# Attention scores of two heads in the two 64-row halves of the array, in phases by query block

## The chip, the cores and the metric

The kernel runs on one core of one Trainium2 chip. The metric is the device time of one execution in microseconds (us). Lower is better.

## What is computed

One block of a transformer: cross-attention with a residual, then a layer of mixed experts with a residual, over 2048 rows of 512. Only the first part matters here. Its rows are channels: `q.reshape(B, 8, 64, 512)` makes every 64 rows one head.

```python
def _L0_xattn_ref(q, k, v, gamma):       # q = layernorm(x), k = v = ctx_2048; B = 4, Dq = 512, L = 512
    h = 8; dq = Dq // h; dv = Dv // h    # 64 channels to a head
    qh, kh, vh = (a.reshape(B, h, 64, 512) for a in (q, k, v))
    qk = einsum('bhdq,bhdl->bhql', qh, kh) / sqrt(64)
    sm = softmax(qk, axis=-1)
    ret = einsum('bhql,bhdl->bhdq', sm, vh).reshape(B, Dv, Lq)
    return gamma * ret
x = x + _L0_xattn_ref(_layernorm(x), ctx_2048, ctx_2048, gamma)
x = x + _L0_ffn_ref(_layernorm(x), router_w, w_gate, w_up, w_down, sw_gate, sw_up, sw_down, shared_gate_w)
```

`_L0_ffn_ref` is a shared expert of width 1408 and the two best of eight experts of width 352.

## The kernel before

**Tiles.** The attention works on 16 tiles of 128 rows. A tile `t` holds two heads, `s` = 0 and 1, of 64 rows each; `k = 2 * t + s` counts heads. The scores of a head are 512 queries by 512 keys: four blocks of 128 queries, each filling one PSUM bank (`bS[0]` to `bS[3]`). After the attention come the shared expert (from about 282 us in the trace) and the routed experts (39 slots); the change leaves both as they are.

**Precision.** Operands of matmuls are fp32r. To keep precision each factor is split into a high and a low part (`kh`, `kl` of the keys; high and low of the queries; `vs[.., 0/1]` of the values; `pth`, `ptl` of the transposed probabilities).

**Scores before.** Each head uses all 128 rows of the array. `qs[s]` holds the high queries in one half of its rows and the low ones in the other; `cd` holds the keys of each head twice, once in each half, and is loaded by two DMAs per tile (L342), on top of the load of `cn`, the same rows in natural layout, from which the values come (L346). Per query block two matmuls of 512 columns are enough: `qs` with `kh` (L1234) and `qs` with `kl` (L1235). That is 16 for a tile, in four groups of four.

**One tile, engine by engine.** Every engine has its own queue, written out by hand in a function `tile`, and works through it in order; an engine stops at a semaphore wait, and with it all that is behind.
- PE (L1297 to L1329): for each head and each `c` of four 128-key chunks, `probs_T` transposes four 128x128 blocks of probabilities into `bT[c % 2]` (L1242), and `times_v` adds three matmuls into `bO` (L1255, L1256, L1258). The groups of scores of the next tile stand between them, and so do `values_T`, `rows_T` (four transposes each) and `logits` (eight narrow passes).
- DVE (L977 on): `maxima` (L925) takes the row maximum of each score bank, `inverse` (L930) the reciprocal of the sums, `probs_lo` (L934) makes `ptl` from `bT` and `pth`, `values_lo` (L918) the low part of the values, `rows_out` (L940) adds the finished attention to the rows, and `bn_stats` (L897) takes the moments.
- ACT (L718 on): `exps` (L681) makes the probabilities from a score bank, `probs_hi` (L687) copies `bT` to `pth`, `values_hi` (L673) and `rows_T` (L693) copy out of `bM`, `normed` makes `xn` (L657) and `x2n` (L661), and `queries_hi` (L668) the high queries, 64 rows at a time.
- POOL (L562 on): `norm_p` (L550) multiplies the probabilities by the reciprocal, `keys_hi` and `keys_lo` (L540, L544) split 128x1024 of keys, `queries_lo` (L533) makes the low queries of a head, and `power` (L521, L523) the scale and shift of a normalisation.
- SP (L401 on) issues the loads and stores of the rows.

**Phases.** In the kernel before, the scores of the next head are made while the present head is transposed and multiplied. Each `pb[s]` (the probabilities of one head, four query blocks) exists once. `probs_T` reads columns of all four query blocks, so the first one of a head waits until `norm_p` has done all four blocks of that head (L1239).

## Time and profile before

| | us |
|---|---|
| median of 3 runs | 990.9 (988.89 to 993.4) |
| span of the profiled execution, first to last instruction | 980.4 |
| what the median has above this span | 10.5 |
| attention, until the first matmul of the shared expert | 281.7 |
| one tile of the attention in the steady part | 15.9 |
| PE busy in the span | 887.9 (91%) |

The profile is of one execution. Its own time by the clock that the median uses isn't given; the difference of 10.5 us between the median and its span is what lies around the span. A row of the timeline gives the start, the duration, the engine, the line, what is written and read, and how many instructions were merged; in brackets stands for how long the engine sat idle before it and what released it. PE's matmuls overlap: a row lasts longer than the time to the next one's start, and the distance of the starts is the rate. On ACT and DVE, too, an instruction starts some 0.1 us before the row ahead of it ends.

### The profile page before, as it was taken

The page shows a single profiled execution, that of the slowest core. Times are in us where ns is not written, and L with a number is a line of the kernel's source. Part 1 is how long each engine was busy: PE and PEld are TensorE (multiplying, and loading weights), DVE is VectorE, ACT ScalarE, POOL GpSimd, SP SyncE. Part 2 cuts the span into 40 slices and gives each one's busy share as a digit, 9 for nine tenths or more (in the row PEclk, how much of TensorE's full clock was granted, in tenths as well). Part 3 has the DMA queues.
Part 4 walks back from the last instruction along what each step waited for, and adds up shares of the span by engine and source line. Part 5 has one row for each costly group of instructions (what it writes and reads, how often), then busy time and mean ns, then how long its engine had stood idle before and what let it go on. Part 6 is the DMA issues. An engine that isn't in the chain of part 4 may idle for free.

```text
span 980.4 us, 14857 instructions
## 1 busy us (share of the span) xinstructions
PE 887.9 (91%) x4560; PEld 743.1 (76%) x4560; DVE 608.1 (62%) x920; ACT 537.9 (55%) x918; POOL 487.4 (50%) x500
## 2 busy tenths in 40 slices
PE   5798999989989999999999999999888888888993
PEld 3587777778777888888888888888777777777882
DVE  5678787878845633421222121258999998999881
ACT  5588878787855321121121111258777777777781
POOL 5687788777610000273100000027777778887774
PEclk9899999999999999999999999999999999999996
DMA  9334434443633323000400055556333333333333
GB/s 138 80 127 132 134 125 137 120 148 109 226 120 117 97 76 128 1 1 25 118 11 1 0 175 177 177 176 209 66 65 64 64 64 64 64 64 64 65 55 43
DMA packets 70143, 93.78 MB, mean 96 GB/s; under 512 B 16137, under 2 KB 35593, under 8 KB 70098
## 3 DMA queue, kind: packets, MB, share of 16 engines
q1 hardware_dynamic: 60338, 72.73, 24.9%
q0 software_dynamic: 9760, 20.49, 12.1%
q8 instruction: 24, 0.39, 0.2%
q14 instruction: 21, 0.17, 0.1%
HBM read 65.59 MB, written 27.60 MB: 95 GB/s over the span
## 4 chain that ended last, share of the span: by engine, by line
PE 43%; POOL 15%; issue 13%; ACT 2%; POOLq 2%; DMA 2%; DVE 1%; SPq 0%; ACTq 0%; DVEq 0%
PE bank L1348 8%; PE bank L1349 8%; PE bank L1350 8%; POOL sidx L615 5%; POOL wd L631 4%; PE bank L1362 4%; PE bank L1364 4%; PE bank L1363 4%; POOL gidx L607 2%; POOL out L624 2%; POOL xg L610 1%; DMA out<-y,sidx 1%; PE bank L1242 1%; ACT pb L681 1%; PE bank L1415 1%
## 5 line engine op out<-in xcount | busy, mean ns | idle before, releaser
L1036 DVE TENSOR_TENSOR sg<-bank,sg 128x512 f32<-128x512 f32 x44 | 30.4, 692 | 208.7 <-PE bank L1350 200.0
L1348 PE MATMUL bank<-x_hl,wsp 128*128 128x512 f32 x352 | 137.1, 390 | 0.0
L1350 PE MATMUL bank<-x_hl,wsp 128*128 128x512 f32 x352 | 137.0, 389 | 0.0
L1349 PE MATMUL bank<-x_hl,wsp 128*128 128x512 f32 x352 | 136.9, 389 | 0.0
L610 POOL DMA_INDIRECT xg<-x_normed_rows,gidx x39 | 40.9, 1048 | 186.9 <-PE bank L1372 158.8
L1152 DVE TENSOR_TENSOR wg<-wex,wg 128x1408 fp32r<-128x1408 f32 x39 | 112.0, 2871 | 12.4 <-ACT wg L813 12.4
L624 POOL DMA_INDIRECT out<-y,sidx x39 | 96.0, 2462 | 38.4 <-POOL sidx L615 18.4
L787 ACT ACTIVATE sg<-bank 128x512 f32<-128x512 f32 x44 | 26.3, 598 | 158.4 <-PE bank L1350 158.4
L687 ACT ACTIVATE pth<-bank 128x512 fp32r<-128x512 f32 x128 | 73.3, 598 | 49.2 <-PE bank L1242 47.7
L593 POOL DMA_INDIRECT slot_rows<-msrc,posi x32 | 32.8, 1025 | 134.2 <-DVE posi L1143 124.7
L934 DVE TENSOR_TENSOR ptl<-bank,pth 128x512 fp32r<-128x512 f32 x128 | 85.9, 682 | 18.7 <-ACT pth L687 18.4
L550 POOL TENSOR_SCALAR pb<-pb,rinv 128x512 f32<-128x512 f32 x128 | 87.3, 696 | 13.3 <-DVE rinv L930 7.8
L794 ACT ACTIVATE hh<-sg 128x512 fp32r<-128x512 f32 x44 | 27.8, 631 | 114.9 <-DVE sg L1036 100.2
L681 ACT ACTIVATE pb<-bank,negmax 128x512 f32<-128x512 f32 x128 | 86.9, 689 | 0.7 <-DVE negmax L925 0.3
L925 DVE TENSOR_REDUCE negmax<-bank 128x1 f32<-128x512 f32 x128 | 82.2, 682 | 0.8 <-PE bank L1235 0.2
L1234 PE MATMUL bank<-kh,qs 128*128 128x512 f32 x128 | 58.8, 459 | 20.7 <-POOL qs L533 17.1
L1350 PEld LDWEIGHTS bank<-x_hl,wsp 128*128 128x128 f32 x352 | 66.1, 188 | 13.7
L1348 PEld LDWEIGHTS bank<-x_hl,wsp 128*128 128x128 f32 x352 | 66.1, 188 | 13.7
L1349 PEld LDWEIGHTS bank<-x_hl,wsp 128*128 128x128 f32 x352 | 66.1, 188 | 13.6
L1242 PE MATMUL bank<-ident,pb 128*128 128x128 f32 x512 | 72.4, 275 | 2.8 <-POOL pb L550 2.8
L848 ACT ACTIVATE wd<-wex 128x1024 fp32r (+1 forms) x39 | 41.3, 1060 | 60.1 <-PE bank L1441 59.3
L1242 PEld LDWEIGHTS bank<-ident,pb 128*128 128x128 f32 x512 | 61.9, 142 | 14.1 <-POOL pb L550 3.8
(160 smaller groups left out, 2420.0 us busy)
## 6 DMA issues: line engine op xcount, KB each, us to landing
cd<-in_ctx SPq DMA_DIRECT2D x32, 256.0 KB, 4.9
wex<-in_L_ffn_w_gate SPq DMA_DIRECT2D x8, 704.0 KB, 4.4
wex<-in_L_ffn_w_up SPq DMA_DIRECT2D x8, 704.0 KB, 5.8
xb<-in_x SPq DMA_DIRECT2D x16, 256.0 KB, 4.7
cn<-in_ctx SPq DMA_DIRECT2D x16, 256.0 KB, 3.0
x2b<-in_x SPq DMA_DIRECT2D x16, 256.0 KB, 2.7
x_rows<-x2b SPq DMA_DIRECT2D x16, 256.0 KB, 2.1
x_normed_rows<-x2n SPq DMA_DIRECT2D x16, 256.0 KB, 2.0
```

The lines of the kernel that those rows point to most:

```text
L550: gp.tensor_scalar(pb[s][:, q, :], pb[s][:, q, :], rinv[:, s, q:q + 1], 0.0, ALU.mult, ALU.add).then_inc(g_pn, 1)
L624: g.indirect_dma_start(out=out, out_offset=bass.IndirectOffsetOnAxis(ap=sidx[j % 4][:, 0:1], axis=0), in_=y3[j % 2][:, :], in_offset=None, ...
L681: sc.activation(pb[s][:, q, :], bS[q][:, :], ACT.Exp, bias=negmax[:, s, q:q + 1], scale=1.0, accum_out=rsum[:, s, q:q + 1]).then_inc(a_exp, 1)
L687: sc.activation(pth[c][:, :], bT[c % 2][:, :], ACT.Copy).then_inc(a_pth, 1)
L925: ve.tensor_reduce(negmax[:, s, q:q + 1], bS[q][:, :], AX_X, ALU.max, negate=True).then_inc(d_max, 1)
L934: ve.tensor_tensor(ptl[c][:, :], bT[c % 2][:, :], pth[c][:, :].bitcast(F32), ALU.subtract).then_inc(d_ptl, 1)
L1152: ve.tensor_tensor(wg3[:, 1, :], wex[:, e, 0:W3], wg3[:, 0, :].bitcast(F32), ALU.subtract).then_inc(d_wg, 1)
L1234: te.matmul(bS[q][:, :], qs[s][:, q * P:(q + 1) * P], kh[par][:, s, :], start=True, stop=False)
L1242: ins = te.transpose(bT[c % 2][:, q * P:(q + 1) * P], pb[s][:, q, c * P:(c + 1) * P], ident[:, :])
L1348: te.matmul(bk[:, :], hi, xhi, start=(h == 0), stop=False)
L1349: te.matmul(bk[:, :], hi, xlo, start=False, stop=False)
L1350: ins = te.matmul(bk[:, :], lo, xhi, start=False, stop=(h == HC - 1))
```

## The change

The scores of both heads are made together, one query block `c` at a time. `kh`, `kl`, `qh` and `ql` hold 128 rows in natural layout, rows 0 to 63 for head 0 and rows 64 to 127 for head 1. A group of scores is six matmuls with 64 contracted rows each: high by high, high by low, low by high, each first for head 0 in the upper rows and then for head 1 in the lower rows, into two banks `bS[2 * (c % 2) + s]`. There are 24 in a tile, in four groups of six. `cd` and its two DMAs per tile are gone; `kh` and `kl` come from `cn` and are 128x512 instead of 128x1024. `xn` is now one buffer, made on POOL (`queries`) instead of ACT; ACT makes `qh` in one 128x512 instruction directly from `xb`, and POOL makes `ql` in one 128x512 instruction. `pb` exists twice for each head, so that a whole tile can be prepared ahead. `negmax`, `rsum` and `rinv` are indexed by query block and then head. `exps`, `maxima`, `inverse` and `norm_p` take the two heads of a query block, and their places in the queues are new; SP issues the load of `cn` for tile `t + 2` first in a tile, ahead of the stores, instead of last.

In the diff below the removed lines of the functions `tile` of POOL, ACT, DVE and PE are left out (they stand in the listing above), as are declarations, the start-up ahead of the first tile, and the definitions that only follow the new shapes.

```diff
                 if there(t + 2):
+                    load_values(t + 2, par)
                     load_x(t + 2, par)
-                    load_keys(t + 2, par)
                 if there(t - 2):
                     store_columns(t - 2, par)
                 if there(t - 1):
                     store_rows(t - 1, 1 - par)
                 if there(t + 1):
                     load_x2(t + 1, i + par, 1 - par)
-                if there(t + 2):
-                    load_values(t + 2, par)
...
+            def queries(t, par):
+
+                wait_ahead(g, g_nmr[0], t + 1)
+                gp.tensor_scalar(xn[:, :], xb[par][:, :], rstd[:, 0, :], nmr[:, 0, :], ALU.mult, ALU.add).then_inc(g_xn, 1)
+
+            def queries_lo(t, par):
+
+                wait_ahead(g, g_xn, t + 1)
+                g.wait_ge(a_qh, t + 1)
+                gp.tensor_tensor(ql[par][:, :], xn[:, :], qh[par][:, :].bitcast(F32), ALU.subtract).then_inc(ql_done, 1)
+                wait_ahead(g, ql_done, t + 1)
...
+            def norm_p(t, par, c):
+
+                wait_ahead(g, d_rinv, 4 * t + c + 1)
+                for s in range(2):
+                    gp.tensor_scalar(pb[par][s][:, c, :], pb[par][s][:, c, :], rinv[:, c, s:s + 1], 0.0,
                                      ALU.mult, ALU.add).then_inc(g_pn, 1)
...
             def tile(t, i, par):
+                if there(t + 1):
+                    norm_p(t + 1, 1 - par, 0)
                 if there(t + 2):
                     keys_hi(t + 2, i + 1, par)
                 if there(t - 1):
                     power(1, t - 1)
                 if there(t + 1):
+                    norm_p(t + 1, 1 - par, 1)
                 if there(t + 2):
                     power(0, t + 2)
+                    keys_lo(t + 2, par)
+                if there(t + 1):
+                    norm_p(t + 1, 1 - par, 2)
                 if there(t + 2):
+                    queries(t + 2, par)
+                    queries_lo(t + 2, par)
+                if there(t + 1):
+                    norm_p(t + 1, 1 - par, 3)
...
+            def queries_hi(t, par):
+
+                act.wait_ge(g_nmr[0], t + 1)
+                after(act, e_s, 8 * t - 8)
+                after(act, ql_done, t - 1)
+                sc.activation(qh[par][:, :], xb[par][:, :], ACT.Identity, bias=nmr[:, 0, :], scale=rstd[:, 0, :]).then_inc(a_qh, 1)
...
+            def exps(t, par, c):
+                after(act, e_t, 8 * t - 8)
+                for s in range(2):
+                    act.wait_ge(d_max, 8 * t + 2 * c + s + 1)
+                    sc.activation(pb[par][s][:, c, :], bS[2 * (c % 2) + s][:, :], ACT.Exp, bias=negmax[:, c, s:s + 1], scale=1.0,
+                                  accum_out=rsum[:, c, s:s + 1]).then_inc(a_exp, 1)
...
                 k = 2 * t
                 probs_hi(k, 0)
                 probs_hi(k, 1)
                 if there(t - 2):
                     rows_T(t - 2, i - 1, par)
                 if there(t + 1):
+                    exps(t + 1, 1 - par, 0)
                 probs_hi(k, 2)
+                if there(t + 1):
+                    exps(t + 1, 1 - par, 1)
                 probs_hi(k, 3)
+                if there(t - 2):
+                    logits(t - 2)
                 if not there(t + 1):
                     tokens_hi(0, 0)
                 k = 2 * t + 1
                 probs_hi(k, 0)
+                if there(t - 1):
+                    rows_normed(t - 1, i - 1 + par, 1 - par)
+                if there(t + 1):
+                    exps(t + 1, 1 - par, 2)
+                if there(t + 2):
+                    queries_hi(t + 2, par)
                 probs_hi(k, 1)
                 if not there(t + 1):
+                    act.wait_ge(a_qh, NT)
+                    act.wait_ge(g_xn, NT)
                     act.wait_ge(e_vt, NT)
                     act.wait_ge(kl_done, NT)
+                    act.wait_ge(e_s, 8 * NT)
                     weights_hi(0)
                 if there(t + 1):
+                    values_hi(t + 1, 1 - par)
                 probs_hi(k, 2)
                 if there(t + 1):
+                    exps(t + 1, 1 - par, 3)
                 probs_hi(k, 3)
                 if not there(t + 1):
                     weights_hi(1)
...
+            def maxima(t, c):
+                for s in range(2):
+                    dve.wait_ge(e_s, 8 * t + 2 * c + s + 1)
+                    ve.tensor_reduce(negmax[:, c, s:s + 1], bS[2 * (c % 2) + s][:, :], AX_X, ALU.max, negate=True).then_inc(d_max, 1)
+
+            def inverse(t, c):
+                dve.wait_ge(a_exp, 8 * t + 2 * c + 2)
+                after(dve, g_pn, 8 * t + 2 * c - 6)
+                ve.reciprocal(rinv[:, c, :], rsum[:, c, :]).then_inc(d_rinv, 1)
...
 
             def tile(t, i, par):
                 k = 2 * t
+                if isinstance(t, int) and t == 0:
+                    inverse(0, 3)
                 if there(t - 1):
                     rows_out(t - 1, i - 1 + par, 1 - par)
                 probs_lo(k, 0)
+                if there(t + 1):
+                    maxima(t + 1, 0)
                 if there(t - 1):
                     dve.wait_ge(d_x2, t)
                     moments(1, t - 1, x2b[1 - par][:, :])
                 probs_lo(k, 1)
                 if there(t - 1):
                     aggregate(1, t - 1)
                 if there(t + 1):
+                    inverse(t + 1, 0)
+                    maxima(t + 1, 1)
                 if there(t - 1):
                     variance(1, t - 1)
                 probs_lo(k, 2)
...
                 probs_lo(k, 3)
                 if not there(t + 1):
                     tokens_lo(0, 0)
+                if there(t + 1):
+                    inverse(t + 1, 1)
                 if there(t + 2):
                     aggregate(0, t + 2)
                 k = 2 * t + 1
+                probs_lo(k, 0)
                 if there(t + 2):
                     variance(0, t + 2)
                 if there(t + 1):
+                    maxima(t + 1, 2)
                 probs_lo(k, 1)
                 if there(t + 1):
+                    values_lo(t + 1, 1 - par)
+                    inverse(t + 1, 2)
+                    maxima(t + 1, 3)
                 probs_lo(k, 2)
                 if not there(t + 1):
                     weights_lo(0)
                 if there(t + 1):
+                    inverse(t + 1, 3)
                 probs_lo(k, 3)
                 if not there(t + 1):
                     weights_lo(1)
...
-            def scores(k, t, par, s, pair):
-
-                if pair == 0:
-                    pe.wait_ge(ql_done, k + 1)
+            def scores(t, par, c):
+
+                if c == 0:
+                    pe.wait_ge(ql_done, t + 1)
                     pe.wait_ge(kl_done, t + 1)
 
-                after(pe, a_exp, 4 * k - 4 + 2 * pair + 2)
-                for q in (2 * pair, 2 * pair + 1):
-                    te.matmul(bS[q][:, :], qs[s][:, q * P:(q + 1) * P], kh[par][:, s, :], start=True, stop=False)
-                    te.matmul(bS[q][:, :], qs[s][:, q * P:(q + 1) * P], kl[par][:, s, :], start=False, stop=True).then_inc(e_s, 1)
-
-            def probs_T(k, s, c):
+                after(pe, a_exp, 8 * t + 2 * c - 2)
+                terms = ((qh, kh), (qh, kl), (ql, kh))
+                for n, (a, b) in enumerate(terms):
+                    for s in range(2):
+                        r = slice(DH * s, DH * (s + 1))
+                        ins = te.matmul(bS[2 * (c % 2) + s][:, :], a[par][r, c * P:(c + 1) * P], b[par][r, :], start=(n == 0), stop=(n == 2))
+                        if n == 2:
+                            ins.then_inc(e_s, 1)
+
+            def probs_T(k, par, s, c):
                 if c == 0:
-                    pe.wait_ge(g_pn, 4 * k + 4)
+                    pe.wait_ge(g_pn, 4 * k + 7 if s == 0 else 4 * k + 4)
                 after(pe, d_ptl, 4 * k + c - 1)
                 for q in range(QC):
-                    ins = te.transpose(bT[c % 2][:, q * P:(q + 1) * P], pb[s][:, q, c * P:(c + 1) * P], ident[:, :])
+                    ins = te.transpose(bT[c % 2][:, q * P:(q + 1) * P], pb[par][s][:, q, c * P:(c + 1) * P], ident[:, :])
                 ins.then_inc(e_t, 1)
...
             def tile(t, i, par):
                 k = 2 * t
+                probs_T(k, par, 0, 0)
+                probs_T(k, par, 0, 1)
+                if there(t + 1):
+                    scores(t + 1, 1 - par, 0)
                 times_v(k, t, 0, par, 0)
+                probs_T(k, par, 0, 2)
+                if there(t + 1):
+                    scores(t + 1, 1 - par, 1)
                 times_v(k, t, 0, par, 1)
+                probs_T(k, par, 0, 3)
                 if there(t - 2):
                     logits(t - 2, par)
                 times_v(k, t, 0, par, 2)
                 k = 2 * t + 1
+                probs_T(k, par, 1, 0)
+                if there(t + 1):
+                    scores(t + 1, 1 - par, 2)
+                times_v(k - 1, t, 0, par, 3)
+                if there(t + 1):
+                    values_T(t + 1, i + par, 1 - par)
+                probs_T(k, par, 1, 1)
                 times_v(k, t, 1, par, 0)
+                probs_T(k, par, 1, 2)
+                if there(t + 1):
+                    scores(t + 1, 1 - par, 3)
                 times_v(k, t, 1, par, 1)
+                probs_T(k, par, 1, 3)
                 times_v(k, t, 1, par, 2)
                 if there(t - 1):
                     rows_T(t - 1, 1 - par)
```

## Rows read from the trace of the kernel before

**Rows 1.** The page, busy time of PE over the span, its share and instructions.
```profile
PE 887.9 (91%) x4560; PEld 743.1 (76%) x4560; DVE 608.1 (62%) x920; ACT 537.9 (55%) x918; POOL 487.4 (50%) x500
```
**Rows 2.** Windows: stretch, its length, busy us of each engine, clock, DMA share, GB/s.
```profile
150.00:200.00 50.00, 46.22 (x274) 38.82 (x273) 40.79 (x88) 41.98 (x97) 40.55 (x50) 1.00 0.41 131
```
**Rows 3.** Timeline of PE, one tile from its first transposes to the next one's.
```profile
153.44 1.03 PE L1242 MATMUL bank<-ident,pb 128*128 128x128 f32 x8
155.60 0.49 PE L1234 MATMUL bank<-kh,qs 128*128 128x512 f32 x1 [1.13 <-POOL qs L533]
155.93 0.39 PE L1235 MATMUL bank<-kl,qs 128*128 128x512 f32 x1
...
156.63 0.39 PE L1255 MATMUL bank<-pth,vs 128*128 128x512 f32 x1
...
157.32 0.60 PE L1242 MATMUL bank<-ident,pb 128*128 128x128 f32 x4
157.67 0.48 PE L1255 MATMUL bank<-pth,vs 128*128 128x512 f32 x1
...
159.81 0.95 PE L1282 MATMUL bank<-rgT,x2T 128*128 128x9 f32 x8
160.62 0.48 PE L1255 MATMUL bank<-pth,vs 128*128 128x512 f32 x1
...
169.38 1.04 PE L1242 MATMUL bank<-ident,pb 128*128 128x128 f32 x8
```
**Rows 4.** Timeline of ACT in the same stretch.
```profile
158.03 0.60 ACT L687 ACTIVATE pth<-bank 128x512 fp32r<-128x512 f32 x1 [0.31 <-PE bank L1242]
...
166.29 0.62 ACT L673 ACTIVATE vs<-bank 128x512 fp32r<-128x512 f32 x1
166.80 0.60 ACT L687 ACTIVATE pth<-bank 128x512 fp32r<-128x512 f32 x1
167.30 0.81 ACT L657 ACTIVATE xn<-xb,nmr,rstd 128x512 f32<-128x512 f32 x1
168.00 0.68 ACT L681 ACTIVATE pb<-bank,negmax 128x512 f32<-128x512 f32 x1
...
168.67 0.69 ACT L681 ACTIVATE pb<-bank,negmax 128x512 f32<-128x512 f32 x1
```
**Rows 5.** Timeline of DVE just behind it.
```profile
169.56 0.17 DVE L930 RECIPROCAL rinv<-rsum 128x2 f32<-128x2 f32 x1 [1.01 <-ACT pb L681]
169.68 1.29 DVE L925 TENSOR_REDUCE negmax<-bank 128x1 f32<-128x512 f32 x2
170.89 0.74 DVE L940 SCALAR_TENSOR_TENSOR x2b<-bank,gam,x2b 128x512 f32<-128x512 f32 x1
171.54 0.68 DVE L934 TENSOR_TENSOR ptl<-bank,pth 128x512 fp32r<-128x512 f32 x1
172.14 0.69 DVE L897 BATCH_NORM_STATS2 stats<-x2b 128x6 f32<-128x512 f32 x1
```
**Rows 6.** Timeline of POOL in the tile of rows 3.
```profile
158.42 1.36 POOL L550 TENSOR_SCALAR pb<-pb,rinv 128x512 f32<-128x512 f32 x2
...
160.91 1.29 POOL L533 TENSOR_TENSOR qs<-xn,qs 64x512 fp32r<-64x512 f32 x1 [0.18 <-POOL nmr L523]
162.41 0.55 POOL L521 TENSOR_TENSOR rstd<-vare,mhalf 128x1 f32<-128x1 f32 x1 [0.21 <-issue]
...
164.70 2.38 POOL L544 TENSOR_TENSOR kl<-cd,kh 128x1024 fp32r<-128x1024 f32 x1
```
**Rows 7.** Timelines: first transposes of tiles 0, 1 and 15; POOL's wait in tile 0.
```profile
20.70 1.09 PE L1242 MATMUL bank<-ident,pb 128*128 128x128 f32 x8 [0.92 <-POOL pb L550]
...
30.55 1.04 POOL L540 TENSOR_SCALAR kh<-cd 128x1024 fp32r<-128x1024 f32 x1 [8.58 <-DMA cd<-in_ctx]
...
41.50 1.03 PE L1242 MATMUL bank<-ident,pb 128*128 128x128 f32 x8
...
266.30 1.03 PE L1242 MATMUL bank<-ident,pb 128*128 128x128 f32 x8
```

220 lines of the change are left out of this document (61 added, 159 removed).

## The prediction, made before the change ran

> **What bounds the kernel now.** I read the page first: PE is busy for 91% of the span [rows 1], so at first sight any matmul saved is time saved. But the change touches only the attention, so that stage has to be read alone. In its steady part PE has 46.2 of 50 us, and DVE, ACT and POOL 40 to 42 each, at a granted clock of 1.00 [rows 2]: four engines stand within some 15% of each other, and then the order of the queues matters as much as the sums. So I went to the timelines. A tile takes 169.38 - 153.44 = 15.94 us [rows 3]. Eight transposes take 0.79 us until the next matmul can start (two groups of four at 0.35, and 0.09), yet the scores start at 155.60, which is 1.37 us later than that: PE waits for the low queries from POOL. PE's own work is 15.94 - 1.37 = 14.57 us per tile. So the present bound is PE, plus one stall that POOL causes.
>
> **Durations taken from the rows**, as the distance of starts. PE [rows 3]: four transposes 0.35; a 512-column matmul 0.23 (0.32 for the first behind transposes); `times_v` 0.69; a group of scores 156.63 - 155.60 = 1.03; `logits` 0.81; a result is there 0.40 after the start of its last matmul. From the start of four transposes to ACT's copy 158.03 - 157.32 = 0.71. ACT [rows 4]: a copy 0.50, a scaled 128x512 copy 0.70, `exps` 0.67 for one head and 1.33 for a pair; the reciprocal can start 169.56 - 168.67 = 0.89 after the second exp's start [rows 4, 5]. DVE [rows 5]: a pair of maxima 1.20, `rows_out` 0.65, a subtraction or statistics 0.60 (its result after 0.69), small ones 0.1. POOL [rows 6]: `norm_p` of two blocks 1.36, a subtraction over 512 columns 1.2 to 1.3 (half of the 2.38, or the 64-row one), 0.2 behind each wait on its own result. Hand-overs between engines cost 0.03 to 0.1 us.
>
> **The change, part by part.** (a) Scores on PE. Sixteen full matmuls become 24 half ones. If the halves run side by side, a group is three steps of 0.23 plus 0.09, or 0.78, against 1.03. The trace has no 64-row matmul and no change between halves and the whole array. I bound a change between 0 and 0.17 us: a matmul lasts 0.40 while the next one starts after 0.23 [rows 3], so emptying the array exposes at most 0.17. I take 0.12, since a real change seems nearer to emptying than to nothing, and two of them per group: a group is 0.78 to 1.12, taken as 1.0. Were the halves one after the other it would be 6 x 0.23 + 0.09 = 1.47, and up to 1.8 with changes. So PE's own work becomes about 14.45 us: this part alone gives almost nothing. (b) The stall of 1.37 us goes, because `ql` of a tile is now made a whole tile ahead. (c) POOL loses about 0.5 + 1.2 us (keys at half the width) and about 1.3 (one `ql` for two), and gains `queries` at 0.68. (d) ACT loses `xn` and two half copies and gets `qh`: 0.70 against some 1.95. (e) DVE has the same work, in another order. (f) Two DMAs of 256 KB per tile go. The load of `cn` moves to the head of SP's queue, past two stores of rows, the store of columns and `load_x2`; it waits there for `e_vt` and `kl_done` of the previous tile, both long past, and behind it only the load of `xb` is queued. The data are first used in the next tile, so this is hidden. In total PE, ACT and POOL all get less to do. The question is what the new order does.
>
> **The walk through one steady tile after the change**, with the first transposes of head 0 at time 0, in the order of the new queues and with the durations above. PE: transposes c0 at 0 and c1 at 0.35, scores block 0 at 0.79 with the result at 1.97, `times_v` c0 at 1.79, transposes c2 2.48, scores block 1 at 2.83 (result 4.0), `times_v` c1 from 3.83. DVE: `rows_out`, `ptl` c0 at 1.33, maxima of block 0 at 1.97 to 3.17, statistics to 3.77, `ptl` c1 to 4.37 (result 4.46), aggregate, reciprocal 0 to 4.55, maxima 1 to 5.75, variance, `ptl` c2 at 5.82 (result 6.51). The last matmul of `times_v` c2 needs it, so it starts at 6.54, and head 1's first transposes at 6.77. ACT copies them at 7.47 to 8.10, DVE subtracts to 8.70 and takes the maxima of block 2 from 8.77 to 9.97 (first result 9.46). ACT now has `exps` 2 from 9.49 to 10.82, then `qh` to 11.52, and only then the copy of head 1's c1, which is there at 12.15. **DVE waits for that copy from 9.97 to 12.15**, because `probs_lo` stands next in its queue; behind it stand `values_lo`, reciprocal 2 and maxima 3. `ptl` c1 to 12.75, `values_lo` to 13.35, reciprocal 2 to 13.44, maxima 3 to 14.64, `ptl` c2 to 15.33. ACT: `exps` 3 from 14.16 to 15.49 and head 1's last copy to 16.12; `ptl` c3 is done at 16.81, the last matmul of the tile starts at 16.84, and PE is free at 17.07. That is one end. POOL has another: `norm_p` 2 waits for reciprocal 2, 13.53 to 14.87; `queries` to 15.6; 0.2; `queries_lo` to 17.0; 0.2; and only then `norm_p` 3, whose first half ends at 17.9. The next tile's first transposes wait for exactly that (seventh `g_pn` of the tile). **So the period is 17.95 us**, 2.0 more than now, with three chains above 15.94: POOL's (17.95), the tile's last `ptl` (17.07), and `exps` 3 directly to `norm_p` 3 without the queries (reciprocal at 15.72, 16.5).
>
> The Trainium skill (TensorEngine Tiling (Array Packing), Key Properties) says that a change of tiling mode drains TensorE. Priced by the row bound of 0.17 for each of the two changes in a group, the two groups ahead of head 1's transposes would put the period near 18.15 and the time near 1016. No run here shows it yet.
>
> **The sum.** Tile 0's first transposes stay near 20.7 [rows 7]. The scores start some 3 us earlier, since `kh` no longer waits for `cd`, but all four query blocks of both heads must then be through exps and `norm_p`: eight exps and seven of eight `norm_p` at 0.67 to 0.68, with `ql` of tile 1 (1.4), `queries` (0.7) and `keys_lo` (1.2) between them, about the same end. Tile 0 now takes 41.50 - 20.70 = 20.8 us, with POOL waiting 8.58 us for `cd` [rows 7]; after the change 1 MB less lies ahead of that load and its data are wanted only about 6 us into the tile, so I take the pure 17.95 and little stall, and tile 1 starts near 38.5: 3.0 us gained (0 to 4). Thirteen tiles (1 to 13) of 17.95 are 233.4, and tile 14, which has no queries of a tile 16 in its queues, about 16.3: tile 15 starts at 288.2 instead of 266.30 [rows 7], 21.9 later. Tile 15 has no scores ahead; I leave it and all behind it as they are (0 to 1 us less). The span becomes 980.4 + 22 = 1002, and with the 10.5 us around it the time is 1013 us, 2.2% above the median of 990.9.
>
> **The rivals.** (1) PE sets the pace and the chains above don't hold. For: PE is the busiest engine now, ACT and POOL get lighter, and the stall goes. The period is then 13.6 (changes free) to 14.5. Against: every link of the walk is an order in a queue. It decides if the copy of head 1's c1 and the last `ptl` come 2.5 us earlier than I have them. Time: 14 x (14.5 - 15.94) - 3 = -23, so 968 us. (2) The halves do not run side by side, so the change doesn't do what it says on PE. A group is 1.5 to 1.8; the two groups ahead of head 1's transposes push these by 1.0 us and the rest follows; period 18.9. Time: 1013 + 13 x 0.95 = 1025 us. No row excludes it. The skill speaks for overlap: the page TensorE: Matmul & The Clock Gate, Part 3, reports 3.07 times for four tiles of 32 rows at 512 columns; by it the group would stay at or below my 1.0. No row of this trace can confirm that. (3) POOL's chain is too long in my walk (the queries finish earlier), and the tile's last `ptl` sets the period at 17.07: 13 x -0.88, so 1001 us. (4) About no change: two chains are over-priced by a microsecond each and the period is 16.0 to 16.3: 988 to 995 us.
>
> **Chances.** The forecast (1005 to 1020) 0.48, (2) and above 0.18, (3) 0.14, (4) 0.08, (1) 0.12. A measurement of this kernel tells about 0.5%, 5 us, from no change. So faster by more than that 0.12, within it 0.08, slower 0.80. For 8 in 10 I leave out (1) and the far end of (2): 988 to 1028.
>
> **What would show each step.** In the profile after: the distance of the first transposes of tiles (17.9 right, 14.5 rival 1, 17.1 rival 3); PE idle before the first transposes of a tile, released by `norm_p`, and before `times_v`, released by `pth` and `ptl`; DVE idle before `ptl` about 2 us per tile, released by ACT; the wait of PE on the low queries gone; the starts of two matmuls of a pair of scores within 0.1 us of each other and pairs 0.23 apart (rival 2: every matmul 0.23 apart); the gap behind a group of scores (a change of mode); a period with less idle time on DVE than 4 us would refute the walk. The prediction would also be wrong if PE's longer pauses (up to 1.6 us by the walk) lowered its granted clock: it is 1.00 now with pauses of 1.4 us, and a fall would make the tile longer still.

## The result, and the profile after

The changed kernel takes 1028.9 us (median of 4 runs, 1025.8 to 1034.0), the kernel before it 992.2 us beside it: a ratio of 1.037, interval 1.033 to 1.042. A later comparison gave 1.033 (1.031 to 1.035). So it is slower by some 33 to 37 us, where 22 us were forecast. The profiled execution has a span of 1032.0 us and a time of 1034.0.

The page first: the row that answers to [rows 1].

```profile
PE 920.8 (89%) x4688; PEld 727.1 (70%) x4688; DVE 612.5 (59%) x918; ACT 520.2 (50%) x886; POOL 459.5 (45%) x502
```

ACT and POOL have less work in all, 18 and 28 us, as the change says, and yet the kernel is slower. PE's busy time is up by 33 us although its work is about the same. Short waits disappear in the modelled ends of matmuls (from 166.25 to 166.64 us the timeline of PE has one step of 0.39 where a step is 0.23, and no idle time beside it), so a PE that is kept waiting a little all the time looks busy. In this one execution PE also paused in the shared expert, with 3.92 us busy and a granted clock of 0.52 from 480 to 490 us; the repeated run of the changed kernel has no such pause, so it is not the change's. The stretch of [rows 2] (same columns) says more:

```profile
150.00:200.00 50.00, 44.12 (x260) 30.55 (x261) 36.10 (x78) 32.78 (x79) 29.29 (x44) 1.00 0.21 73
```

Every engine was less busy in these 50 us, at a granted clock of 1.00: PE 44.1 for 46.2, DVE 36.1 for 40.8, ACT 32.8 for 42.0, POOL 29.3 for 40.6. Nobody is the bound; everybody waits. For whom, the table of waits tells (engine and line that waited, line that it waited for, us in total, times, longest; stretch of 75 to 295 us, twelve tiles):

```profile
POOL pb L542 <- DVE rinv L912: 83.4, 36, 4.3
DVE ptl L916 <- ACT pth L675: 49.1, 48, 2.2
...
ACT pb L669 <- DVE negmax L907: 33.3, 48, 1.1
...
PE bank L1229 <- POOL pb L542: 11.0, 12, 1.0
```

PE's wait for POOL's low queries, the stall of 1.13 us in [rows 3], is gone. In its place stands a ring: POOL waits for DVE's reciprocals, DVE for ACT's copy, ACT for DVE's maxima, and PE, at the head of each tile, for POOL. The timelines show one turn of it (start, duration, engine, line, operation, count, idle time before and its releaser). PE, from a tile's first transposes to the next one's:

```profile
153.54 1.09 PE L1229 MATMUL bank<-ident,pb 128*128 128x128 f32 x8 [0.99 <-POOL pb L542]
...
156.25 0.60 PE L1229 MATMUL bank<-ident,pb 128*128 128x128 f32 x4
156.78 0.50 PE L1220 MATMUL bank<-kh,qh 64*128 64x512 f32 x2
157.11 0.39 PE L1220 MATMUL bank<-kl,qh 64*128 64x512 f32 x2
157.34 0.40 PE L1220 MATMUL bank<-kh,ql 64*128 64x512 f32 x2
157.67 0.50 PE L1242 MATMUL bank<-pth,vs 128*128 128x512 f32 x1
...
169.09 0.51 PE L1245 MATMUL bank<-ptl,vs 128*128 128x512 f32 x1 [1.04 <-DVE ptl L916]
...
172.10 1.09 PE L1229 MATMUL bank<-ident,pb 128*128 128x128 f32 x8 [1.00 <-POOL pb L542]
```

A tile takes 172.10 - 153.54 = 18.56 us, for 15.94 in [rows 3]. The scores do go in pairs, three steps of 0.33, 0.23 and 0.33 us. But the group costs 157.67 - 156.78 = 0.89, and the way into it 156.78 - 156.25 = 0.53 where four transposes gave way after 0.35 in [rows 3]. That is 0.18 us for going into the 64-row mode and, 0.89 against my 0.78, 0.11 for coming out of it: 1.07 in all, against 1.03 for a group before. By the records the packing gives nothing on PE.

ACT, DVE and POOL in the second half of the same tile:

```profile
163.90 0.68 ACT L669 ACTIVATE pb<-bank,negmax 128x512 f32<-128x512 f32 x1
...
164.56 0.81 ACT L650 ACTIVATE qh<-xb,nmr,rstd 128x512 fp32r<-128x512 f32 x1
165.27 0.59 ACT L675 ACTIVATE pth<-bank 128x512 fp32r<-128x512 f32 x1
```
```profile
162.51 1.28 DVE L907 TENSOR_REDUCE negmax<-bank 128x1 f32<-128x512 f32 x2
165.89 0.69 DVE L916 TENSOR_TENSOR ptl<-bank,pth 128x512 fp32r<-128x512 f32 x1 [2.10 <-ACT pth L675]
166.50 0.68 DVE L901 TENSOR_TENSOR vs<-bank,vs 128x512 fp32r<-128x512 f32 x1
167.10 0.16 DVE L912 RECIPROCAL rinv<-rsum 128x2 f32<-128x2 f32 x1
167.17 1.27 DVE L907 TENSOR_REDUCE negmax<-bank 128x1 f32<-128x512 f32 x2
```
```profile
167.43 1.36 POOL L542 TENSOR_SCALAR pb<-pb,rinv 128x512 f32<-128x512 f32 x2 [2.19 <-DVE rinv L912]
168.77 0.76 POOL L519 TENSOR_SCALAR xn<-xb,rstd,nmr 128x512 f32<-128x512 f32 x1
169.68 1.28 POOL L525 TENSOR_TENSOR ql<-xn,qh 128x512 fp32r<-128x512 f32 x1
171.27 1.36 POOL L542 TENSOR_SCALAR pb<-pb,rinv 128x512 f32<-128x512 f32 x2 [0.31 <-POOL ql L525]
```

On ACT the second exp of block 2 and the high queries stand ahead of the copy of head 1's second transposes. DVE idles 2.10 us for that copy. The reciprocal of block 2, an instruction of 0.16 us whose input was ready near 164.8, stands two places further down and starts at 167.10. POOL idles 2.19 us for it, then does `norm_p` 2, the queries, the low queries and only at 171.27 `norm_p` 3, for which PE waits.

The start of tiles 0, 1 and 15, for [rows 7]:

```profile
20.91 1.97 PE L1229 MATMUL bank<-ident,pb 128*128 128x128 f32 x8 [4.97 <-POOL pb L542]
...
41.08 1.97 PE L1229 MATMUL bank<-ident,pb 128*128 128x128 f32 x8 [0.41 <-POOL pb L542]
...
300.06 1.03 PE L1229 MATMUL bank<-ident,pb 128*128 128x128 f32 x8
```

Tile 15 starts 33.8 us later than before, and the shared expert behind the attention starts 35.3 us later (317.0 for 281.7). That is the size of the whole measured loss. The spans of the two profiled executions differ by more, 51.6 us: 16.3 of them lie behind the attention, where both kernels run the same code (715.0 us for 698.7). In the repeated run of the changed kernel that part took 701.4, and in the other runs of this document, all with the same code there, 696 to 716. So I don't count it as the change's. In the repeated run the shared expert starts at 313.3, 31.6 later than before.

### The profile page after: what moved, and what is told of

Read it like the earlier page. It is cut to its first block, busy times and chain, and to the rows that moved or that the text cites. A ratio compares the mean times of both kernels' runs of the same rounds, so it can differ in the third digit from the quotient of the medians.

```text
span 1032.0 us, 14928 instructions
## 1 busy us (share of the span) xinstructions
PE 920.8 (89%) x4688; PEld 727.1 (70%) x4688; DVE 612.5 (59%) x918; ACT 520.2 (50%) x886; POOL 459.5 (45%) x502
## 4 chain that ended last, share of the span: by engine, by line
PE 39%; POOL 14%; issue 13%; DMA 2%; POOLq 2%; ACT 1%; DVE 1%; SPq 0%; DVEq 0%; ACTq 0%
PE bank L1335 8%; PE bank L1337 8%; PE bank L1336 8%; POOL sidx L608 5%; POOL wd L624 4%; PE bank L1349 4%; PE bank L1351 4%; PE bank L1350 4%; POOL gidx L600 2%; POOL out L617 2%; DMA out<-y,sidx 1%; POOL xg L603 1%; PE bank L1229 1%; POOLq L624 0%; DMA stg<-in_L_ffn_sw_down 0%
## 5 line engine op out<-in xcount | busy, mean ns | idle before, releaser
L1335 PE MATMUL bank<-x_hl,wsp 128*128 128x512 f32 x352 | 139.1, 395 | 3.9 <-issue 3.7
L1337 PE MATMUL bank<-x_hl,wsp 128*128 128x512 f32 x352 | 138.7, 394 | 2.7 <-issue 2.7
L1336 PE MATMUL bank<-x_hl,wsp 128*128 128x512 f32 x352 | 138.8, 394 | 1.4 <-issue 1.3
L603 POOL DMA_INDIRECT xg<-x_normed_rows,gidx x39 | 40.8, 1046 | 187.3 <-PE bank L1359 159.3
L1135 DVE TENSOR_TENSOR wg<-wex,wg 128x1408 fp32r<-128x1408 f32 x39 | 116.7, 2992 | 12.6 <-ACT wg L796 12.6
L1229 PE MATMUL bank<-ident,pb 128*128 128x128 f32 x512 | 78.1, 282 | 16.9 <-POOL pb L542 16.9
L1229 PEld LDWEIGHTS bank<-ident,pb 128*128 128x128 f32 x512 | 64.0, 145 | 31.7 <-issue 13.5
L1335 PEld LDWEIGHTS bank<-x_hl,wsp 128*128 128x128 f32 x352 | 67.0, 190 | 18.9 <-issue 5.3
L1337 PEld LDWEIGHTS bank<-x_hl,wsp 128*128 128x128 f32 x352 | 66.9, 190 | 17.2 <-issue 3.3
L1336 PEld LDWEIGHTS bank<-x_hl,wsp 128*128 128x128 f32 x352 | 67.0, 190 | 17.0 <-issue 3.2
L1245 PE MATMUL bank<-ptl,vs 128*128 128x512 f32 x128 | 56.8, 444 | 17.7 <-DVE ptl L916 17.7
```

The source lines that it names most:

```text
L1135: ve.tensor_tensor(wg3[:, 1, :], wex[:, e, 0:W3], wg3[:, 0, :].bitcast(F32), ALU.subtract).then_inc(d_wg, 1)
L1229: ins = te.transpose(bT[c % 2][:, q * P:(q + 1) * P], pb[par][s][:, q, c * P:(c + 1) * P], ident[:, :])
L1245: te.matmul(bO[:, :], hi, ptl[c][:, :], start=False, stop=last).then_inc(e_pv, 1)
L1335: te.matmul(bk[:, :], hi, xhi, start=(h == 0), stop=False)
L1336: te.matmul(bk[:, :], hi, xlo, start=False, stop=False)
L1337: ins = te.matmul(bk[:, :], lo, xhi, start=False, stop=(h == HC - 1))
```

## The experiments

To size the steps I repeated the walk of the prediction for several tiles in a row, with every duration from this trace: changes of mode 0.18 and 0.11, a hand-over of 0.2 us to POOL and 0.04 to the others, the low queries 1.28 and 0.31 behind them. It gives 18.49 us per tile for the changed kernel, and the name "queue walk" below means this sum for other orders of the queues. The period of a kernel is read off as the mean distance of `queries` on POOL over three to five tiles near 150 us. Each ratio is against the kernel before, timed on the same chip.

**Do the halves depend on the order of issue?**

```diff
-                for n, (a, b) in enumerate(terms):
-                    for s in range(2):
+                for s in range(2):
+                    for n, (a, b) in enumerate(terms):
```

> The changed kernel with one difference: the six matmuls of a group of scores go out as three of head 0 and then three of head 1, so that neighbours share their 64 rows and only one pair of six can overlap. Everything else stays. If halves overlap only when neighbours differ (my reading of pairs starting together), a group grows from 0.89 us by 0.37 to 0.46 us, and by the walk through the queues the tile grows from 18.5 by about 0.65 us: about +9 us, 1038 us. Rival (TensorE's own work is what made the change slow): four groups cost their full 1.5 to 1.8 us per tile, +21 to +26 us, 1050 us or more. If order does not matter to the overlap: no change.

Ratio 1.035 (1.029 to 1.041), period 18.57: no change. The timeline of PE shows the reason:

```profile
151.24 0.50 PE L1220 MATMUL bank<-kh,qh 64*128 64x512 f32 x2
151.58 0.40 PE L1220 MATMUL bank<-kl,qh 64*128 64x512 f32 x2
151.81 0.40 PE L1220 MATMUL bank<-kh,ql 64*128 64x512 f32 x2
152.14 0.50 PE L1242 MATMUL bank<-pth,vs 128*128 128x512 f32 x1
```

Although the three matmuls of head 0 are issued ahead of the three of head 1, the records still show them in pairs, and the group still takes 0.90. That the other order reached the chip shows in one thing: the two starts of a pair are 10 nanoseconds apart in the records of this run, in the median, and 3 in the changed kernel. So this gave no serial control; that took another kernel.

**What is the overlap worth?** Both heads' six matmuls in rows 0 to 63:

```diff
-                        r = slice(DH * s, DH * (s + 1))
+                        r = slice(0, DH)
```

> The changed kernel, but the scores of both heads use rows 0 to 63 of the operands (head 1's scores are left out, head 0's stand in both places), so the six matmuls of a group share one half of the array and cannot run side by side. Issue order, banks and all waits stay. If the halves really run in parallel in the changed kernel, a group now takes six steps of 0.23 us instead of three, 0.69 us more, so the distance from the first transposes of one tile to the next goes from 18.56 to about 20.1 us (queue walk with a group of 1.79 us instead of 1.10), and the time rises by about 14 x 1.5 = 21 us, to a ratio near 1.058 against the kernel before. Rival: the pairs of the changed kernel only look simultaneous in the records and the array is shared in time: then the starts go on in steps as they are now, and period and time stay at 18.56 and 1.037. Second rival: two matmuls into the same rows also run side by side because each uses half the rows: same outcome as the first rival, but with pairs still starting together.

```profile
152.41 0.72 PE L1220 MATMUL bank<-kh,qh 64*128 64x512 f32 x2
152.97 0.62 PE L1220 MATMUL bank<-kl,qh 64*128 64x512 f32 x2
153.44 0.63 PE L1220 MATMUL bank<-kh,ql 64*128 64x512 f32 x2
153.99 0.51 PE L1242 MATMUL bank<-pth,vs 128*128 128x512 f32 x1
```

No two matmuls of this group start together in the records. The group takes 1.58 instead of 0.89, the period is 19.95 us and the ratio 1.060 (1.058 to 1.062), 26 us above the changed kernel beside it. The overlap of the halves is real. The second rival of the prediction priced its absence at 0.95 us a tile; it costs 1.39.

**Are the changes of mode what is lost?** In the changed kernel's own order, a group of scores as four matmuls over 128 rows:

```diff
-                terms = ((qh, kh), (qh, kl), (ql, kh))
+                terms = ((qh, kh), (ql, kh))
...
-                        ins = te.matmul(bS[2 * (c % 2) + s][:, :], a[par][r, c * P:(c + 1) * P], b[par][r, :], start=(n == 0), stop=(n == 2))
+                        ins = te.matmul(bS[2 * (c % 2) + s][:, :], a[par][:, c * P:(c + 1) * P], b[par][:, :], start=(n == 0), stop=(n == 1))
```

> The changed kernel in its own order, with each group of scores as four matmuls over the whole 128 rows, as in the kernel before, instead of six over 64 rows (the products mix the heads and the middle term is left out, so the scores are not those of the reference). It prices the change of mode and the packing where the queues set the pace. Theory: a group of 1.03 without a change of mode instead of 1.07 with one moves every transpose by less than 0.1 us, and the chain through ACT's copy, DVE's wait, the reciprocal and POOL has its own length: queue walk 18.49 in both cases, so 18.4 to 18.6 us a tile and a ratio of 1.030 to 1.037. Rival: the changes of mode push the two groups ahead of head 1's transposes late and so make 0.2 of the 0.6 us by which a tile exceeds the forecast, then 18.3 to 18.4 and 3 us less; or they are worth more than the records of PE show, and the period falls towards the forecast 17.95.

```profile
157.30 0.60 PE L1228 MATMUL bank<-ident,pb 128*128 128x128 f32 x4
157.66 0.71 PE L1219 MATMUL bank<-kh,qh 128*128 128x512 f32 x2
158.20 0.63 PE L1219 MATMUL bank<-kh,ql 128*128 128x512 f32 x2
158.67 0.39 PE L1241 MATMUL bank<-pth,vs 128*128 128x512 f32 x1
```

From the transposes to `times_v` it is 158.67 - 157.30 = 1.37 us, for 157.67 - 156.25 = 1.42 with the pairs. The period is 18.49 for 18.56, the ratio 1.031 (1.028 to 1.034). Here it makes next to no difference how the scores are computed (0.07 us of the 2.6 that a tile lost): the loss does not lie in the packing.

**The order of the three lighter engines' queues.** Four edits of the changed kernel, each in one queue.

(1) `norm_p` of block 3 ahead of the queries, on POOL:

```diff
-                if there(t + 2):
-                    queries(t + 2, par)
-                    queries_lo(t + 2, par)
-                if there(t + 1):
-                    norm_p(t + 1, 1 - par, 3)
+                if there(t + 1):
+                    norm_p(t + 1, 1 - par, 3)
+                if there(t + 2):
+                    queries(t + 2, par)
+                    queries_lo(t + 2, par)
```

> The changed kernel with norm_p of query block 3 moved ahead of queries and queries_lo in POOL's queue. My prediction held that POOL's chain (queries, queries_lo, then norm_p 3) sets the period and that without it the next end is 0.9 us earlier: tile 17.6, about -13 us, 1016 us. The rival, from the walk with the trace of the changed kernel: the low queries are wanted by the first scores right at the start of the next tile, so they only move the wait from the transposes to the scores, and the tile gets 19.0 us: +7 us, 1036 us, with PE idle before the scores, released by ql.

Ratio 1.040 (1.034 to 1.045), period 18.8 us. The wait did not go away, it changed its object:

```profile
151.92 1.03 PE L1228 MATMUL bank<-ident,pb 128*128 128x128 f32 x8
154.34 0.50 PE L1219 MATMUL bank<-kh,qh 64*128 64x512 f32 x2 [1.38 <-POOL ql L525]
```

The transposes come on time and the scores behind them wait for the low queries. Those are needed right behind the first eight transposes, so POOL's chain up to the queries has to end early, whatever the order of its last two steps.

(2) The queries ahead of `norm_p` of block 2, where POOL stands idle anyway:

```diff
-                if there(t + 1):
-                    norm_p(t + 1, 1 - par, 2)
-                if there(t + 2):
                     queries(t + 2, par)
                     queries_lo(t + 2, par)
                 if there(t + 1):
+                    norm_p(t + 1, 1 - par, 2)
                     norm_p(t + 1, 1 - par, 3)
```

> The changed kernel with one move, in POOL's queue: queries and queries_lo stand ahead of norm_p of block 2 instead of behind it. They fit into the time in which POOL waits for the reciprocals of block 2. This takes the queries out of the chain reciprocal 2, norm_p 2, queries, queries_lo, norm_p 3, and tests the third rival of the forecast (the last ptl of a tile sets the period). Queue walk: period 17.16 us instead of 18.49, time lower by 14 x 1.33 = 18 us, ratio about 1.019. If PE or the chain through DVE's wait for ACT's copy sets the period by itself, the move gives nothing: 18.5 and 1.037. If queries_lo then holds back norm_p 2 because the high queries come late from ACT, the result lies between.

Ratio 1.020 (1.018 to 1.022), period 17.53: 14 us less than the changed kernel beside it.

(3) One reciprocal, ahead of the `ptl` that waits for ACT's copy:

```diff
+                    inverse(t + 1, 2)
                 probs_lo(k, 1)
                 if there(t + 1):
                     values_lo(t + 1, 1 - par)
-                    inverse(t + 1, 2)
                     maxima(t + 1, 3)
```

> The changed kernel with one instruction of 0.08 us moved in DVE's queue: the reciprocal of block 2 stands ahead of the ptl of head 1's second transposes instead of behind it and values_lo. In the changed kernel it stands behind a ptl that waits for ACT's copy, behind exps 2 and the high queries; norm_p 2, the queries, the low queries and norm_p 3 on POOL all follow it. Theory: without that detour POOL's chain ends 1.9 us earlier and the tile's last ptl sets the period: queue walk 17.08 us instead of 18.49, ratio about 1.018. PE's wait for norm_p ahead of a tile's first transposes should vanish (17 us in all now), DVE's wait for ACT's copy should stay (about 2 us a tile). Rival: DVE's idle time itself, not what is queued behind it, sets the period, then the move gives nothing: 18.5 and 1.033 to 1.037.

Ratio 1.020 (1.016 to 1.025), period 17.46. Moving an instruction of 0.16 us takes 1.1 us off each tile. In the waits (75 to 295 us) PE's wait for POOL has shrunk from 11.0 to

```profile
PE bank L1227 <- POOL pb L542: 0.2, 1, 0.2
```

and DVE's for ACT's copy is 25.0 for 49.1, less than I had expected to remain.

(4) That reciprocal and the maxima of block 3 both ahead of it:

```diff
+                    inverse(t + 1, 2)
+                    maxima(t + 1, 3)
                 probs_lo(k, 1)
                 if there(t + 1):
                     values_lo(t + 1, 1 - par)
-                    inverse(t + 1, 2)
-                    maxima(t + 1, 3)
```

> The changed kernel with two steps moved in DVE's queue: reciprocal 2 and maxima 3 of the next tile go ahead of probs_lo of head 1's chunk 1, into the 2.1 us in which DVE waits for that chunk's copy. PE's work is the same. If the order of the queues is what makes the change slow, the tile falls from 18.5 to about 16.6 us: -27 us, 1002 us. Rival (PE's changes between half and whole array, eight a tile, or the 24 matmuls are the cause): no change beyond 3 us, 1029 us.

Ratio 1.014 (1.009 to 1.020), period about 17.0 us (the walk 16.6). One reciprocal and a pair of maxima further up in one queue give back some 20 of the 33 to 37 us.

**All four queues in another order.** Same instructions, same banks and buffers, no wait left out: POOL does the keys first and the low queries ahead of `norm_p` 3, ACT makes its copies in twos ahead of the exps, DVE takes maxima and reciprocals ahead of the `ptl` that would wait, PE puts a group of scores ahead of a tile's first transposes and the `times_v` of head 1 at the end.

```diff
             def tile(t, i, par):
+                if there(t + 1):
+                    scores(t + 1, 1 - par, 0)
-                k = 2 * t
-                probs_T(k, par, 0, 0)
-                probs_T(k, par, 0, 1)
+                probs_T(2 * t + 0, par, 0, 0)
+                probs_T(2 * t + 0, par, 0, 1)
                 if there(t + 1):
-                    scores(t + 1, 1 - par, 0)
+                    scores(t + 1, 1 - par, 1)
...
```

> The same instructions as the changed kernel, with the queues of DVE, ACT, POOL and PE all put in a new order, so that nothing PE waits for is late: scores and maxima early in the tile, head 0's work in between, values late. If order alone is the cause, the tile comes near PE's own work, 14.9 us by the walk: 14 x -3.6 = -51 us, 978 us, which would be faster than the kernel before by 14 us. Rival (PE's work with the changeovers is already above 15.9 us a tile): not below 992 us.

Ratio 0.987 (0.982 to 0.993), and 0.985 (0.981 to 0.989) in a second comparison, for which I had written:

> The kernel with all four queues reordered again, as the control beside the two built on it, on the same chip: period 15.1 us, ratio 0.985 to 0.99 against the kernel before.

The period is 15.10 in both. By the windows PE never stops:

```profile
150.00:200.00 50.00, 50.00 (x320) 38.45 (x320) 43.92 (x95) 41.19 (x95) 37.49 (x57) 1.00 0.30 106
```

This is the changed kernel faster than the one before, by 1.3 to 1.5%. It also makes PE the bound, so here the price of the scores can be measured in time. Four matmuls over 128 rows in this order (the diff of the scores is the one above):

> The kernel with all four queues reordered (14.85 us by the walk, 15.10 measured), but a group of scores is four matmuls over the whole 128 rows, two per bank, as in the kernel before, instead of six over 64 rows; the operands stay the two heads' natural ones, so the products mix the heads and the middle term is left out: the scores are not those of the reference. It prices the packing where PE sets the pace. Theory: six half matmuls in pairs cost 3 x 0.23 + 0.09 plus 0.18 going in and 0.11 coming out, 1.07 to 1.10 us a group, four whole ones cost 1.03 and no change of mode, so the period falls by 0.2 to 0.3 us, to 14.8 to 14.9, and the time by 3 to 4 us against the same orders with packing: packing alone buys nothing on PE and all of the gain of that kernel comes from the queues. Rival: packing pays on PE by three steps instead of four (0.23 a group): the period rises by 0.9 and the time by 13 us.

Ratio 0.979 (0.974 to 0.983) against 0.985 beside it, period 14.80 against 15.10. The 0.3 us a tile is somewhat more than the 4 x 0.05 = 0.2 read off the records; the rival, that packing pays 0.23 a group, is out. The two ratios' intervals overlap, so that whole matmuls are faster here rests on the periods.

**Fewer changes of mode.** Scores of blocks 0 and 1 back to back, and of 2 and 3, all queues ordered around them:

```diff
-                    scores(t + 1, 1 - par, 0)
...
-                    scores(t + 1, 1 - par, 1)
+                    scores(t + 1, 1 - par, 0)
+                    scores(t + 1, 1 - par, 1)
```

> The groups of scores of query blocks 0 and 1 back to back, and those of 2 and 3 (the four score banks hold two groups), with all four queues ordered anew around them. Only two stretches of 64-row matmuls per tile are left instead of four. If each stretch costs 0.18 us going in and 0.11 us coming out plus 0.09 for its first matmul, PE saves about 2 x 0.38 = 0.76 us a tile: queue walk 14.14 us against 14.85 for single groups, so the period should come to 14.3 to 14.5 (the walk has been 0.2 to 0.4 short), and the time to some 9 us below that of the single groups, ratio 0.975 to 0.98. If the changes of mode cost nothing, PE's work stays as it is and the period cannot fall below 15.0: ratio 0.985 to 0.99. If longer stretches of scores starve ACT and DVE of their transposes, it rises above.

Ratio 0.998 (0.995 to 1.001): the forecast failed. The tiles are of uneven length, most between 15.1 and 17.8 us. PE's records of the scores did what was expected. The waits (75 to 250 us) have one that the walk had not:

```profile
DVE stats L875 <- DMA xb<-in_x: 16.5, 10, 2.3
```

In this order DVE's statistics of the next rows stood first in its queue, and the load of those rows had not landed. My walk had no DMA in it. The next run has the statistics behind the fourth `ptl`. Many other steps of all four queues moved with them (the cut shows the statistics alone), so the run tests the new order as a whole:

```diff
             def tile(t, i, par):
...
-                if there(t + 2):
-                    first_norm(t + 2, i + 1, par)
...
                 probs_lo(2 * t + 0, 3)
...
+                if there(t + 2):
+                    first_norm(t + 2, i + 1, par)
```

> The scores in two stretches of two groups per tile again, but with DVE's statistics of the next rows behind the fourth ptl instead of first in its queue, where in the run before they waited for the load of those rows (16.5 us in all), and the queues ordered again under that condition. Theory: the saving on PE (0.37 us for each two groups put together, as that run's records show) is real and was eaten by that wait: queue walk 14.1 us, so a period of 14.2 to 14.5 against 15.10 for single groups, time 9 to 12 us below these, ratio 0.972 to 0.978. Rival: two groups back to back make ACT and DVE late whatever stands first, since for 1.6 us PE makes no transposes: the period stays above 15.1, the ratio at 0.985 or more.

```profile
160.06 0.50 PE L1212 MATMUL bank<-kh,qh 64*128 64x512 f32 x2
160.40 0.39 PE L1212 MATMUL bank<-kl,qh 64*128 64x512 f32 x2
160.63 0.40 PE L1212 MATMUL bank<-kh,ql 64*128 64x512 f32 x2
160.86 0.39 PE L1212 MATMUL bank<-kh,qh 64*128 64x512 f32 x2
...
161.65 0.50 PE L1234 MATMUL bank<-pth,vs 128*128 128x512 f32 x1
```

Two groups take 161.65 - 160.06 = 1.59, and one way in of 0.18: 1.77 for what cost 2 x 1.07 = 2.14. The period is 14.56 us, the ratio 0.975 (0.972 to 0.978), the fastest of all that ran. 15.10 - 14.56 = 0.54 of the 0.74 expected from two such pairs arrive in the time. Since the rest of the queues differs too, no run shows how much of the 0.54 is the changes of mode, nor that the wait for the load alone had spoiled the run before.

**The start.** Is tile 0 long because PE is slow there? 26 transposes that nobody reads, in PE's idle time before it:

```diff
             scores(0, 0, 3)
+            for w in range(26):
+                te.transpose(bT[0][:, (w % QC) * P:(w % QC + 1) * P], ident[:, :], ident[:, :])
```

> The changed kernel with 26 transposes of the identity, whose result nobody reads, put on PE ahead of tile 0, where PE is idle from 15.9 to 20.9 us. Theory: tile 0 takes 20.2 us instead of the forecast 17.95 because its first 5.8 us of matmuls run at half rate (0.43 us per step instead of 0.23) after that idle stretch; with PE busy, the steps at the start of tile 0 are 0.23 us and tile 1 starts 1 to 2.5 us earlier than 41.1. The total falls by the same 1 to 2.5 us. Rival: tile 0 is long for another cause, such as a wait on a load; then tile 1 starts at 41 as now, whatever the step. A second one: the idle stretch has nothing to do with the rate at which tile 0 begins, and the steps stay at 0.43 us.

with the changed kernel itself as the control:

> The changed kernel itself, as a control beside the three variants on the same chip: ratio 1.037 against the kernel before, tiles 18.56 us apart, tile 0 starting at 20.9 and tile 1 at 41.1 us.

```profile
15.32 3.06 PE L1284 MATMUL bank<-ident 128*128 128x128 f32 x26
21.01 1.09 PE L1229 MATMUL bank<-ident,pb 128*128 128x128 f32 x8 [2.62 <-POOL pb L542]
...
40.18 1.97 PE L1229 MATMUL bank<-ident,pb 128*128 128x128 f32 x8 [0.48 <-POOL pb L542]
```

The control's tile 0 starts at 21.00, with the eight transposes at half rate (1.97 us), and its tile 1 at 40.90. With the warm start the eight transposes go at full rate, but after them the granted clock falls to 0.57 and only at 25.8 are the steps 0.23 again, for 26.5 in the control. PE is at half rate for about 3.8 us of tile 0 instead of about 5.5. By estimate 1.7 us less at half rate are worth half of that, 0.85 us; tile 0 is 19.2 us instead of 19.9, 0.7 us less. Over the whole kernel nothing is left of it: 1.034 (1.031 to 1.038) against 1.033. The profiled execution lost more in tile 1 than it had gained: there its clock fell again, and tile 1 took 20.4 us for 18.0 in the control.

The control differs in one more thing. In it PE is at half rate already ahead of the idle stretch (steps of 0.43 from its first scores at 8.4 us on), while the execution with the warm start had reached the full rate at 12.4, before the added transposes. The run with `norm_p` 3 first, which starts as the changed kernel does, had the full rate from 12.2 us on too, and after its idle stretch it was at half rate:

```profile
14.80 0.40 PE L1219 MATMUL bank<-kh,ql 64*128 64x512 f32 x2
20.83 1.97 PE L1228 MATMUL bank<-ident,pb 128*128 128x128 f32 x8 [5.64 <-POOL pb L542]
```

So the idle stretch of 5.6 us ended at half rate even from the full rate, and with the added work it did not. Each is one execution.

## Why the prediction was wrong in its size

The direction, the place and the mechanism were right: the ring in the queues that the walk describes is there, and edits to it give the time back. What was wrong is the length of the ring, 18.56 us instead of 17.95, and to a smaller part the start. Step by step, with the first transposes of the tile at 0:

- **The stall of PE goes, its own work stays.** Right in effect, wrong in the reason. I wrote that `ql` is made a whole tile ahead; its start of 16.14 and 1.28 us put it 1.1 us ahead of the next tile's first transposes and about 2 us ahead of the scores that need it. One edit on POOL brought the wait back at once (1.38 us), so there is little room. PE's own work, put at 14.45 us, was put too low: in the kernel where PE never stops the tile takes 15.10. That did no harm here, as PE is not the bound.
- **Group of scores taken as 1.0, change of mode bounded by 0.17.** It is 1.07, with 0.18 going in and 0.11 coming out: inside the group's range of 0.78 to 1.12, the way in just above its bound. The Trainium skill (TensorEngine Tiling (Array Packing), Key Properties) says that a change of tiling mode drains TensorE. The records fit that, 0.53 for 0.35 us ahead of the scores and 0.89 for 0.78 behind them; what the engine does in that time they don't show.
- **DVE's wait for ACT's copy, 9.97 to 12.15.** In the trace from 10.2 to 12.35: 2.10 us for the 2.18 of the walk.
- **POOL's chain.** `norm_p` 2 at 13.53, measured 13.89; queries 14.87, measured 15.23; low queries 15.8, measured 16.14; `norm_p` 3 at 17.2, measured 17.73; period 17.95, measured 18.56. **This is the step that failed in size.** Some 0.2 us was there when the copy came, since head 1's first transposes were already 0.2 late (at 6.96). 0.16 came at POOL, which started 0.33 us after the start of the reciprocal, 0.18 in the walk. Another 0.2 came between the low queries and `norm_p` 3 (1.59 from start to start, for 1.4), and 0.1 at the hand-over to PE. In my walk a hand-over between engines cost 0.03 to 0.1. From the end of the reciprocal to POOL's start it is 0.17 (0.33 from start to start). POOL's wait for its own low queries I took as 0.2, from the small instructions of [rows 6]; it is 0.31, and the trace of the kernel before had it, behind a subtraction of the same kind:

```profile
171.63 1.37 POOL L550 TENSOR_SCALAR pb<-pb,rinv 128x512 f32<-128x512 f32 x2 [0.33 <-POOL qs L533]
```

  Taking away the changes of mode moved the period by only 0.07, so they are not the cause. The prediction's other estimate, 18.15 us by two changes of mode, was nearer in number, but for a reason that the run with whole matmuls contradicts: there the changes are gone and the tile still takes 18.49.
- **The three chains.** I named POOL's chain as the longest (17.95) and the last `ptl` as the next (17.07, the third rival). Two independent edits that take POOL's chain out, the queries moved and the reciprocal moved, leave 17.53 and 17.46. The gap between the chains was 0.88 in the walk and is 1.0 to 1.1 in the runs. That it is the last `ptl` which ends last there is the walk's word; no run takes it out.
- **Tile 0 and tile 1.** Tile 1 was forecast at 38.5 and starts at 41.08. I took the pure period for tile 0. It takes 20.17: after PE's 4.97 us of idle time its steps are 0.43 instead of 0.23 us until about 26.5. I had read [rows 7] for times and not looked at the clock that a longer idle stretch would leave behind, though I named it at the end of the prediction as what could go wrong. The warm start shows 0.7 us of it and that the delay passes on to tile 1. What was left at half rate there, 22.0 to 25.8, costs PE another 1.9 us by estimate (half of that stretch), which would cover the rest, but no run took that away.
- **Tile 15** was left as before (15.4) and takes 17.0: a wait of 1.71 us for a `ptl`, over at 309.99, then steps at half rate until 313. In the repeated run the same wait of 1.71 us is not followed by a fall, and the tile takes 15.7.
- **The sum.** Against the forecast of +22 us, the profile has +35.3 at the start of the shared expert: tile 1 starts 2.6 late, tiles 1 to 14 add 9.3 (259.0 for 249.7; 2.4 of it is tile 1 alone, at half clock), tile 15 adds 1.6. The repeated run has fewer falls of the clock and is the cleaner witness, +31.6: 2.4 at tile 1, 7.0 in tiles 1 to 14, 0.3 in tile 15. So some 7 of the 10 us that the forecast lacks there are the length of the ring, and 2.4 are tile 0.
- **The 10.5 us around the span** are none. In the profiled execution after, time and span differ by 2.0. The profiled execution of before was simply quicker than the timed ones. The forecast carried the 10.5 on both sides, so its difference of 22 us is not touched.

As for the rivals: PE sets the pace (968 us) is in kind what the same instructions give in another order, 15.10 us a tile and a ratio of 0.985 to 0.987, or 976 to 978 us on the median before. The change did not bring that order with it. The halves not overlapping is refuted by the two runs on it.

One point stays open. The walk is short by 0.4 us in the three kernels with a step moved up on DVE or POOL (17.08 for 17.46, 17.16 for 17.53, 16.6 for 17.0), by 0.07 in the changed kernel itself, and 0.2 too long with `norm_p` 3 first (19.0 for 18.8). I have no row that says which hand-over it is.

## What to carry to other kernels

When all engines but one get lighter, the order in which they serve each other decides: find every instruction that waits, and see what short instruction with a ready input stands behind it and for whom that one is. A reciprocal of 0.16 us moved over two places gave 13 us or more, and the same work ordered anew turned a ratio of 1.035 into 0.985. Packing small matmuls into halves of the array did not pay in stretches of three pairs (1.42 us for 1.37), and does by the records in stretches of six (1.77 for 2 x 1.03); so group them. Before a consumer is moved to the head of a queue, look when its load lands.

## What the runs showed of the hardware

- **The two 64-row halves run side by side whatever the order of issue.** Three matmuls of one half issued ahead of three of the other were recorded in pairs, 151.24, 151.58 and 151.81, and the group took the same 0.90 us as with the pairs issued together. Only the distance within a pair grew, from 3 to 10 nanoseconds. The Trainium skill (TensorE: Matmul & The Clock Gate, Part 3) says that matmuls start and end strictly in the order of the program; the records and the time of this run speak against that across halves.
- **A change between 64 and 128 rows costs 0.18 us in and 0.11 us out**, 0.29 for the two, in the packed groups at full clock; with six matmuls that save 0.25 against four whole ones, that cancels the packing (1.42 for 1.37 us).
- **Half rate at the same place in one execution and not in another.** Two profiled executions of the changed kernel entered tile 1 after nearly the same idle times (0.41 and 0.59 us just ahead of it). One had the granted clock at 0.50 from 42 to 46 us, the 1.2 GHz level, and its tile 1, from 41.08 to 61.49, took 20.4 us; the other stayed at 1.00, and its tile took 18.0. The end of tile 1 in the first and both ends in the second:

```profile
61.49 1.09 PE L1229 MATMUL bank<-ident,pb 128*128 128x128 f32 x8 [0.52 <-POOL pb L542]
```
```profile
40.90 1.09 PE L1229 MATMUL bank<-ident,pb 128*128 128x128 f32 x8 [0.59 <-POOL pb L542]
58.93 1.09 PE L1229 MATMUL bank<-ident,pb 128*128 128x128 f32 x8 [0.52 <-POOL pb L542]
```

In both, PE had also waited 1.05 and 0.3 us within the four microseconds before. The warm start's execution fell at that place too, after waits of 1.05, 0.28 and 0.48 us, and that of the run with the heads in turn did not. What decides between the two, no run here shows.
- At the start of tile 0 the column of the granted clock reads 1.00 while the steps are 0.43 us, the same as at 42 to 46 us where it reads 0.50. There the steps are the better witness.
